# A gated cross-attention block with a routed feed-forward on one core: attention values in one block per batch, and a re-spread of the routing map, the first steps and the row lists

## The reference

```
q = layernorm(x) @ Wq + bq          # 16 heads of 16
k, v = ctx @ Wk + bk, ctx @ Wv + bv
attn = softmax(q k^T / 4) v         # per head, 112 x 375 scores
x = x + tanh(g_xattn) * (attn @ Wo + bo)
xf = layernorm(x).reshape(3584, 256)
scores = softmax(xf @ w_router.T)   # 8 experts, top 2 per row
h = silu(xf @ w1[e]) * (xf @ w3[e]) # 352 wide
x = x + tanh(g_ffn) * sum over the row's 2 experts of weight * (h @ w2[e])
```

## Time and profile before

| | us |
|---|---|
| median of 3 runs | 913.42 |
| runs | 908.33 to 919.16 |
| the profiled execution, device time | 914.7 |
| its span, first to last instruction | 912.8 |
| mean granted TensorE clock | 0.979 of full speed |
| busy: PE, PEld, DVE, ACT, POOL | 868.9, 689.5, 495.1, 423.0, 475.3 |

### The profile page before, as it was taken

One profiled execution on the slowest core, in us unless ns is written; L12 is line 12 of the kernel. 1 busy time (PEld: TensorE's weight loads), 2 busy tenths in 40 slices (PEclk: granted clock), 3 DMA queues, 4 the chain that ended last, 5 costly groups with the idle time before them and its releaser, 6 DMA issues.

```text
span 912.8 us, 21112 instructions
## 1 busy us (share of the span) xinstructions
PE 868.9 (95%) x7209; PEld 689.5 (76%) x7209; DVE 495.1 (54%) x1161; ACT 423.0 (46%) x1086; POOL 475.3 (52%) x565
## 2 busy tenths in 40 slices
PE   7799999999999999999998999889998999999995
PEld 6578888888888888888877888766776777777773
DVE  3456666866775875776687786562541222222221
ACT  2246556565655565556554565454422222222221
POOL 6244443454455445545544455344677565656652
PEclk9899999999999999999999999988999999999998
DMA  6756666777768667557654566425434343443432
GB/s 159 156 142 168 165 168 158 172 168 185 170 157 198 144 139 165 135 124 170 138 136 110 130 153 138 94 77 186 65 59 59 59 68 60 65 69 59 62 61 29
DMA packets 99631, 112.27 MB, mean 123 GB/s; under 512 B 28860, under 2 KB 80820, under 8 KB 99528
## 3 DMA queue, kind: packets, MB, share of 16 engines
q1 hardware_dynamic: 79144, 92.33, 43.0%
q0 software_dynamic: 18240, 16.83, 11.9%
q10 hardware_dynamic: 2144, 1.77, 0.9%
HBM read 35.48 MB, written 17.53 MB: 58 GB/s over the span
## 4 chain that ended last, share of the span: by engine, by line
PE 83%; DMA 6%; DVE 3%; issue 3%; another core or an unknown queue 1%; ACT 1%; POOL 1%; ACTq 1%; POOLq 0%; DVEq 0%
PE ps L1267 16%; PE ps L1044 11%; PE ps L1050 9%; PE ps L1015 9%; PE ps L1327 9%; PE ps L1029 9%; PE ps L1055 7%; DMA stack<-negmax_t 5%; PE ps L1192 3%; PE ps L1151 2%; PE ps L1286 2%; DVE negmax L785 2%; PE ps L1231 1%; PE ps L1070 1%
## 5 line engine op out<-in xcount | busy, mean ns | idle before, releaser
L785 DVE TENSOR_REDUCE negmax<-ps 112x2 f32<-112x750 f32 x256 | 240.5, 939 | 160.4 <-PE ps L1044 155.9
L523 ACT ACTIVATE probs<-ps 125x448 f32<-125x448 f32 x384 | 208.4, 543 | 238.5 <-PE ps L1015 224.7
L1015 PE MATMUL ps<-stack 97*125 97x224 f32 x768 | 194.2, 336 | 6.8 <-DMA stack<-negmax_t 6.3
L356 POOL DMA_DIRECT2D stack<-negmax_t x128 | 69.4, 544 | 241.2 <-ACT negmax_t L581 232.6
L1015 PEld LDWEIGHTS ps<-stack 97*125 97x125 f32 x768 | 131.8, 191 | 32.5 <-DMA stack<-negmax_t 9.1
L1044 PE MATMUL ps<-stack 96*112 96x376 f32 x512 | 143.6, 361 | 8.0 <-DVE negmax L785 7.7
L446 POOL DMA_INDIRECT out_dram<-y,idx x63 | 100.5, 1595 | 78.5 <-PE ps L1231 23.4
L623 ACT ACTIVATE silu<-ps 128x352 f32<-128x352 f32 x63 | 29.2, 463 | 187.0 <-PE ps L1267 171.7
L971 DVE TENSOR_TENSOR h<-silu,ps 128x352 f32<-128x352 f32 x63 | 32.8, 520 | 145.0 <-PE ps L1267 127.7
L1050 PE MATMUL ps<-wv_sb,ctx_t 128*125 128x256 f32 x384 | 102.4, 390 | 0.2 <-DVE bo_gated L836 0.2
L1029 PE MATMUL ps<-probs,v_sb 125*32 125x112 f32 x3072 | 101.3, 265 | 0.0
(11 more groups left out here) (204 smaller groups left out, 1212.5 us busy)
## 6 DMA issues: line engine op xcount, KB each, us to landing
stack<-split SPq DMA_DIRECT2D x252, 150.0 KB
ctx_t<-in_ctx_dram SPq DMA_DIRECT2D x32, 375.0 KB, 4.7
stack<-split SPq DMA_DIRECT2D x126, 94.0 KB
stack<-split SPq DMA_DIRECT2D x126, 56.0 KB
out_dram<-xa SPq DMA_DIRECT2D x32, 112.0 KB, 4.3
xn_scratch<-xn SPq DMA_DIRECT2D x32, 112.0 KB, 3.8
xa<-in_x_dram SPq DMA_DIRECT2D x7, 448.0 KB, 5.7
w_sb<-in_L_ffn_w_dram SPq DMA_DIRECT2D x8, 352.0 KB
```

Source lines behind the costliest of these rows:

```text
L356: gp.dma_start(dst[:, :, SKP + SQ * h:SKP + SQ * h + SQ], negmax_t[4 * h:4 * h + 4, half, :].bitcast(f32)).then_inc(s_nmrow[half][c % NSLO ...
L523: act.activation(probs[:, g % 2, ch, :], ps[0:KW, EXPB + k % 2, 0:4 * SQ], ACT.Exp).then_inc(s_exp, 1)
L785: dve.tensor_reduce(negmax[:, half, :, p4], ps[0:SQ, m1:m2 + 1, 0:SK], axis=AX.X, op=ALU.max, negate=True).then_inc(s_max, 1)
L1015: last = pe.matmul(ps[0:KW, EXPB + k % 2, QW * m:QW * m + QW], stack[:, place_of(b), p, KW * ch:KW * ch + KW], stack[:, place_of(b), p, SK ...
```

## The change

1. `values(e, 0..3)` stand together at k = 1 of the next step, 48 matmuls in a row, behind `exps` and `maxes` of that place. `probs` becomes a ring of 14 chunks. The stationary operand is cut from 32 to 17 columns; the other rows of the PSUM bank are zeroed once at the start.
2. The second half's `negmax_turn` (PE) and `negmax_out` (ACT) stand ahead of `exps(b, 1)`.
3. `maxes` and their reductions stand at k = 0, 1, 2, 3, 5, 7, 9, 10; at k = 5 behind the query projection. The transposes of `pv_t` move from k = 3 to k = 4.
4. `early_map` has twelve parts, at k = 1, 5, 8 of steps 24, 25, 28 and 29; `route`'s parts are spread over two steps.
5. Start: SP and POOL, not ACT, send batch 0's `stack`; batch 2's keys and queries are made ahead of step -1 (`third_batch`); batch 0's maxima use two pairs of banks in turn; the output bias is worked out inside step -1.
6. Feed-forward: 16 row lists instead of 8 (semaphores in 8), loaded two steps later; `place` is left out of every fourth tile's turn, so its 16 calls take 21 tiles.

```diff
-        v_sb = sb("v_sb", [KW, NSLOT, KC, HEADS, 32])
+        v_sb = sb("v_sb", [KW, NSLOT, KC, HEADS, HD + 1])
-        probs = sb("probs", [KW, 2, KC, 4 * SQ])
+        NP = 14
+        probs = sb("probs", [KW, NP, 4 * SQ])
+        MAX_IN = (0, 1, 2, 3, 5, 7, 9, 10)
+        MAP_STEPS = [GB * SNAP + n for n in (8, 9, 12, 13)]
         def max_banks(c, t):
+            if c == 0 and t % 2:
+                return EXPB, EXPB + 1
...
+            def stack_first():
+                src, dst = split[:, 0, :, :].bitcast(f32), stack[:, place_of(0), :, :].bitcast(f32)
+                gp.wait_ge(s_qlo, 1)
+                gp.wait_ge(s_khi, DC)
...
-                if 0 <= t - 1 < 2 * GB * TOP:
-                    place(NU - 2 + (t - 1) // (GB * TOP), (t - 1) % (GB * TOP) // TOP, (t - 1) % TOP)
+                n = t - 1 - t // 4
+                if t % 4 < 3 and 0 <= n < 2 * GB * TOP:
+                    place(NU - 2 + n // (GB * TOP), n % (GB * TOP) // TOP, n % TOP)
...
                 for k in range(12):
+                    if k == 1 and b is not None and b > 0:
+                        negmax_out(b, 1, BB_)
                     if b is not None:
-                        g, ch = k // 3, k % 3
-                        act.wait_ge(s_exp_ps, 12 * b + k + 1)
-                        if ch == 0:
-                            wait(act, s_pv, 4 * b + g - 1)
-                        act.activation(probs[:, g % 2, ch, :], ps[0:KW, EXPB + k % 2, 0:4 * SQ], ACT.Exp).then_inc(s_exp, 1)
+                        n, reader = 12 * b + k, 12 * b + k - NP
+                        act.wait_ge(s_exp_ps, n + 1)
+                        if reader >= 0:
+                            act.wait_ge(s_pv, reader // 3 + 1)
+                        act.activation(probs[:, n % NP, :], ps[0:KW, EXPB + k % 2, 0:4 * SQ], ACT.Exp).then_inc(s_exp, 1)
...
                 for k in range(12):
-                    if b is not None:
-                        exps(b, k)
-                    if k == 1 and e is not None:
-                        values(e, 3)
-                    if k % 3 == 1 and k > 1 and b is not None:
-                        values(b, k // 3 - 1)
-                    if k % 3 != 2 and c is not None:
-                        maxes(c, k // 3 * 2 + k % 3)
...
+                        if b is not None and b > 0:
                             negmax_turn(b, 1, BB_)
+                    if b is not None:
+                        exps(b, k)
+                    if k in MAX_IN and k != 5 and c is not None:
+                        maxes(c, MAX_IN.index(k))
+                    if k == 1 and e is not None:
+                        for g in range(4):
+                            values(e, g)
...
             for i in range(FIRST, LAST):
+                step(i)
+                if i == -2:
+                    third_batch()
                 if i == -1:
-                    pe.wait_ge(s_wr_t, 1)
-                step(i)
+                    negmax_turn(0, 1, PVB)
...
                 if t == 0:
-                    values(B - 1, 3)
+                    for g in range(4):
+                        values(B - 1, g)
```

More of the change, by code:

```diff
@@ L309, in _ @@
                         load_w2(c)
+                    for t in range(NIS, NI):
+                        load_idx(t)
             store_xn2(B - 2)
@@ L321, in _ @@
                     sp.sem_inc(s_met_sp, 1)
-                if t + NI < TILES:
-                    load_idx(t + NI)
+                    for n in range(EARLY, NI + GATE - 3):
+                        load_idx(n)
+                elif t > GATE and t + NI - 4 < TILES:
+                    load_idx(t + NI - 4)
         @block.gpsimd
@@ new lines, in step @@
+                    if settled is not None and k == 7:
+                        route(settled, 4)
+                    if settled_in(i - 1) is not None and k == 2:
+                        route(settled_in(i - 1), 5)
+                if i == -2:
+                    for m in range(DC):
+                        dve.wait_ge(s_khi, 2 * DC + m + 1)
+                        dve.scalar_tensor_tensor(out=split[:, 0, m, KLO:KLO + SK], in0=ps[:, BB_ if m else BC, 0:SK], scalar=bk_sb[:, m:m + 1],
+                                                 in1=split[:, 0, m, KHI:KHI + SK].bitcast(f32), op0=ALU.add, op1=ALU.subtract).then_inc(s_klo, 1)
@@ L876, in early_map, with added @@
+            def added(out, parts, n):
+                link(dve.tensor_reduce(out[:, 0:n], parts[:, 0:n, :], axis=AX.X, op=ALU.add))
             def early_map(part):
@@ L1041, in maxes @@
                 else:
-                    wait(pe, s_max, 8 * c + t)
+                    wait(pe, s_max, 8 * c + t - (1 if c == 0 else 0))
                 for h in range(2):
@@ L1135, in step @@
                         key_proj(a, 0, BC)
-                    if k == 3 and e is not None:
+                    if k == 4 and e is not None:
                         if s is not None:
@@ L1154, in step @@
                     if k == 5 and c is not None:
+                        maxes(c, MAX_IN.index(k))
+                    if k == 5 and c is not None and c > 0:
                         if e is not None:
```

422 lines of the change are left out of this document (258 added, 164 removed).

## The result

The changed kernel takes 885.06 us (median of 4 runs, 882.32 to 888.39) against 915.25 for the kernel before beside it (908.33 to 919.16): ratio 0.968, 95% interval 0.961 to 0.975. The forecast was 876, with a range of 855 to 893. The profiled execution is the slowest of the four, with 888.39 us and a span of 886.7, at a mean granted clock of 0.98. Against the span before of 912.8 that is 26.1 us less (30.2 by the medians), where the sum of the prediction had 37.2 us.

The account below looks back on a forecast made before the run. The prediction took PE's instruction list to bound the long middle. Its terms, -29.8 - 3.8 + 13.5 - 3.4 - 7.3 - 3.5 - 2.9, sum to -37.2 us: 914.7 to 877.5 profiled, 876 as median, range 855 to 893.

Parts of the forecast that it names:

- One block of values: Values groups on PE: three of four groups a batch lose their borders, 96 x 0.31 us, -29.8 us.
- The new stall: Second maxes of a step: PE waits for DVE's reduction, 0.45 us in each of 30 steps, +13.5 us.
- `route` over two steps: Spreading route's parts over two steps: no effect, since it waits for nobody on the path.
- The map: Step 24: early_map in twelve small parts no longer holds up a reduction PE waits for, -3.4 us.
- The turn in front: Turn of the maxima moved earlier: PE's ten waits for the maxima's DMA go, -3.8 us.
- The start: Before the first exps: less DMA waiting and faster maxima, first exps at 41.5 to 42 us, -7.3 us.
- The seam: Last step to feed-forward: most of the 2.54 us DMA wait and values groups go, block enters tile 0, -3.5 us.
- The tiles: Feed-forward: leaving out every fourth place keeps POOL from falling behind PE, -2.9 us.
- (a): Rival at the second maxes: no new stall appears, 862.5 us; chance 0.15.
- (b): Rival: the stall is twice as long, or ACT stalls too, or the start gives half, 889 us; chance 0.2.
- (c): Rival on values: the 0.31 us belong to each group, not to the border, 906 us; chance 0.07.
- (d): Rival: maxes at denser places outruns its one pair of banks, 66 us more, 942 us; chance 0.06.

Follow-up runs that it names:

- e5_stats_moved: Changed kernel with the second pair of layer-norm statistics and halve1 at step 4n+2 instead of 4n+3; 872.65 us, ratio 0.9611.
- e6_gates_moved: Changed kernel with only route's part 4 moved, from k = 7 to k = 1 of the next step; 873.22 us, ratio 0.9609.
- e11_seam: Changed kernel with ACT's copy, xn, statistics, route and halve1 moved, and loads of w3_hi and w2 behind the last maxima's wait; 856.05 us, ratio 0.9409.
- e3_narrow: Kernel before with only the values' stationary operand cut from 32 to 17 columns; 905.3 us, ratio 0.9972.
- e12_best: As e11_seam, with w3_hi in front of the maxima's wait again and xn before the first reduction in steps -1 and 0; 855.24 us, ratio 0.9423.
- e2_four_blocks: Changed kernel with the values' four groups apart, transposes and exps between them, three borders a step more; 906.65 us, ratio 0.9985.

## Why the prediction came out as it did

The direction and the range were right, and the forecast 9 us low. (The ends of the range are stated a little lower than their own terms give: 856.6 and 895.8.) By its steps, in the profiled execution:

1. **One block of values, -29.8: right.** 0.30 and 0.88 us for one and three borders against the 0.31 and 0.93 forecast. The distances between starts in the two traces say the same: a group was entered after 0.20 us and left after 0.19, where an `exps` and its `maxes` lie 0.11 apart: 0.28 for each group taken out of the way, 90 times in the steps 1 to 30. The 0.096 us a round doesn't follow from its row ((0.57 - 0.26) / 3 is 0.10), but it is what the block of the changed kernel takes (0.575 / 6).
2. **17 columns, 0: right** within what can be told (at most 0.1 us a step).
3. **The new stall, 13.5 at the second `maxes`: the size is right, the place is wrong, and a second wait was missed.** I followed DVE's list and not ACT's. The 0.7 us of `values` that stood ahead of `value_proj(s, 2)` had covered ACT's copy as well. In the changed kernel this wait costs 0.48 us from start to start (10.6 us in all) and 0.10 more behind L1151, and it hides the stall of 0.29. Both together hold 17.16 - 16.58 = 0.58 us in a usual step, some 17 us in 30.
4. **"`route` over two steps: nothing, it waits for nobody on the path": wrong, and the dearest error.** It waits for nobody, but part 4 stands at k = 7 between two reductions, in front of statistics that had been left there. The 13.6 us that e5_stats_moved and e6_gates_moved gained are this term, about half of them by the clock (by the medians of the separate sets it is 12). I gave no figure for DVE's room at k = 7 and never laid out a step of the kind 4n+3. The order of the two kernels shows the pile. Where `halve1` meets POOL it doesn't show, but that it can be held was in the trace of before (2.42 us at 476.29).
5. **The map, -3.4: right.** Step 24 takes 17.2 us, with 16.96 busy.
6. **The turn in front, -3.8: about half.** PE waited 1.8 us (3 times) for this DMA instead of 3.8. At step 12 the rows still landed late. In e5_stats_moved and e6_gates_moved no such wait is left ahead of the seam, so this rest too goes with the large waits.
7. **The start, -7.3: right**, 7.05. The first `maxes` were 2.7 us earlier than forecast (29.23), and lost it to the output bias between the `maxes`, at half clock. On top, step 0 got shorter by 2.2 us (14.2 instead of 16.4), of which nothing was said: its three groups of values (3 x 0.71) stand in step 1 now.
8. **The seam, -3.5: wrong in both its parts.** The +1.9 in it falls behind the first feed-forward matmul; up to there the forecast was -5.4, and it was -1.6 (from 17.6 to 16.1). "Most of it goes" for the wait of 2.54 was wrong: an earlier turn is no help when the transfer then stands behind 2.4 MB of weights. e11_seam shows that. The -3.2 took three groups out of the last step (1.28 + 1.28 + 0.71, though the text names two), but the block puts batch 30's in their place: 2.43 us where one group of 0.71 stood. The three groups' time is missing in step 0 instead (item 7).
9. **The tiles, -2.9: right in size by chance.** The part took 2.5 us less (287.2 to 284.6), but only against an execution that waited. Against e3_narrow, which runs the old feed-forward in 281.0, it took 3.6 us more, and that is tile 0: from the values to the next piece are 4.59 us there, where one group took 0.71. The same 96 records take 2.43 in e12_best; the changed kernel idles between them. First the changed kernel, then e12_best:

```profile
603.63 1.45 PE L1128 MATMUL ps<-probs,v_sb 125*17 125x112 f32 x49
605.47 0.26 PE L1128 MATMUL ps<-probs,v_sb 125*17 125x112 f32 x1 [0.39 <-issue]
...
608.22 0.86 PE L1400 MATMUL ps<-w_lo,xg_t 128*128 x2
```

```profile
571.42 2.50 PE L1134 MATMUL ps<-probs,v_sb 125*17 125x112 f32 x96
573.85 0.86 PE L1406 MATMUL ps<-w_lo,xg_t 128*128 x2
```

The profile names no releaser for this idle time, and its cause is open. What the list of `place` is worth can't be told from zero by these runs.

10. **The order of the other pieces, not in the sum: some -8.** e2_four_blocks has the values as far apart as the kernel before, and the wait for the copy (0.58 us) on top. Without that wait its usual step would be 17.46 us, 0.3 less than the 17.77 of before. Two distances show where it is. The query projection is followed after 0.82 us, and after 1.08 in the kernel before, where the turn of the maxima stood behind it (first before, then after); and PE's two turns take 0.06 us a step instead of 0.25, while the `value_proj` in front of one takes 0.19 more.

```profile
126.44 1.05 PE L1151 MATMUL ps<-xn_t,wq_sb 128*128 128x112 f32 x8
127.52 0.26 PE L1060 MATMUL ps<-ident,negmax 112*8 112x112 f32 x1
```

```profile
116.98 1.05 PE L1256 MATMUL ps<-xn_t,wq_sb 128*128 128x112 f32 x8
117.80 0.57 PE L1145 MATMUL ps<-stack 96*112 96x376 f32 x2
```

The narrower operand can be up to 0.1 us of it (e3_narrow); no run puts the old order back, so the split is read from distances and not tested.

Summed up: from `exps(1, 0)` to `exps(31, 0)` the kernel got 12.8 us faster. By starts in the two traces that is 90 x 0.28 = 25.2 for the borders and some 10.5 for the irregular waits of before at turn, `maxes` and behind values (step 24 among them), less 25.2 for waits that are new (12.3 at `maxes`, 10.6 at `value_proj`, 2.3 at `exps(b, 0)`). The remaining 2.3 is a balance: some 8 from the order, less what the lower clock costs (10.2 us more of it in this stretch than before, at half speed at most 5.1), and small rests. The start gave 7.1, step 0 2.2, the seam 1.6, the rest 2.5: 26.1 in all. Put into the prediction's sum of -37.2, what failed comes to +13.6 (`route`, the pile and its clock), +3.5 (two stalls, 17 instead of 13.5), +3.8 (seam), -1.5 (feed-forward, -2.5 instead of 1.9 - 2.9), -2.2 (step 0) and -8 (order): some -28, with 26.1 measured. So part of the closeness is luck: errors of 21 us one way met 12 the other way.

Of the rivals, (a), no new stall, wasn't the case: at the second `maxes` PE waits for nothing, but only since the other wait covers it. (b) had nearly the size (889): that ACT stalls too, which it named, is so, but the pile-up at k = 7 is not in it. (c) and (d) are out: the `maxes` at k = 2, 3 and 5 wait for nothing in a usual step.

## What to carry to other kernels

When a piece of work is taken out of the bottleneck engine's list, look at every engine that had used it as cover, not only at the busiest one, and follow each buffer that the next instruction writes to its last reader. A step moved off the path is not free where it lands: lay out the fullest step of the cycle, since steps that carry a two- or four-step extra decide, and here waits of 1.7 us cost about as much again in clock. A small transfer on the path must be issued before the bulk, or the bulk must wait for it.
